# Two experts in halves of 128 rows: four output buffers, gathers spread over more gaps, fillers on TensorE ahead of three halves

## The chip, the cores and the metric

The kernel runs on one core of one Trainium2 chip. The metric is the device time of one execution in microseconds (us); lower is better. All times below are from runs and from one profiled execution of the kernel before.

## What is computed

The input x has 2 sequences of 1024 tokens with 128 channels. A layer norm, a two-level wavelet transform with linear attention, and a residual sum give x1. A second layer norm gives the rows h, on which a mixture of 16 experts and one shared expert work. The change touches the experts alone:

```
scores = sigmoid(h @ gate_w.T);  cap = ceil(T / E * TOP_K)   # T = 2048, E = 16, cap = 256
topk_score, topk_ids = top_k(scores.T, cap)                  # each expert picks 256 tokens
xin = h[topk_ids]
up = xin @ up_w.T + up_b;  g = xin @ gw.T + gb               # 128 -> 512, in 4 pieces of 128
eo = (silu(g) * up) @ down_w.T + down_b                      # 512 -> 128
out = zeros.at[topk_ids].add(eo * topk_score);  x = x + out + shared
```

Everything is fp32. An expert picks its own 256 tokens, so that two experts can have the same token: their sums into the output must not run at once.

## The kernel before

The kernel is written out by engine; each engine works through its own list in order, and semaphores order the engines. The first part (wavelet, attention, norms, the choice of 256 tokens for each expert, the shared expert) leaves a table h_rows in HBM (128 channels and 16 scores for each token), a table of row numbers in SBUF (rows, 2 x 128 for each expert), and the output in HBM with x and the shared expert's part.

Then come the experts. For expert e:

- GpSimd (POOL) issues two indirect DMAs that gather 128 rows each into gath (`gather(e, c)`, L525), c = 0 and 1. There are 7 buffers (GBUF); s_gath of the buffer counts both.
- TensorE (PE) turns the two chunks (`turn_x`, L1396) into a PSUM bank; VectorE (DVE) copies the 128 x 256 result to SBUF (`keep_x`, L1065).
- Four pieces j of 128 hidden features, numbered q = 4e + j through all experts: TensorE makes up (L1439) and gate (L1440), 256 columns each, ScalarE (ACT) the silu (L736), VectorE the product with the up part (L1091), and TensorE, two pieces later (LAG), the down product of each chunk (`down(q)`, L1414).
- VectorE adds the bias into eo (`add_bias`, L1075), ScalarE multiplies each chunk by the token's score (`weigh`, L560), and POOL issues two indirect DMAs that add the rows into the output (`scatter(e)`, L536).

eo has two buffers; `add_bias(e)` waits until scatter e-2 has landed. `scatter(e)` waits until scatter e-1 has landed.

In the steady part `turn_x(e+1)` stands in the middle of expert e (after j = 2), so that TensorE goes from one expert to the next without a gap. Only the last expert is different: at q = FINAL (60) TensorE first does the last two downs of expert 14, then `turn_x(15)`, and VectorE does `add_bias(14)` and `keep_x(15)` there.

The order on POOL is written out by hand: 12 gathers (experts 0 to 5), and then scatter 0, BETWEEN[0] gathers, scatter 1, BETWEEN[1] gathers, and so on. With the old BETWEEN (2 seven times, 1 six times, 0) the gathers of expert 13 stand behind scatters 7 and 8, those of expert 14 behind scatters 9 and 10, and those of expert 15 behind scatters 11 and 12.

`stay_warm(n, bank)` (L1112) issues n matmuls of 128 columns of the identity matrix into a bank that nobody reads; each fp32 matmul is two instructions in the trace, here as everywhere.

Of the kernel before, what the change touches and what calls it, by code (L numbers as in the profile page):

```python
# [11 lines left out]
ALU = mybir.AluOpType  # L12
# [9 lines left out]
P = 128  # L22
# [5 lines left out]
def wavelet_attention_moe(nc, x, packed, weights, shared, down_b, out):  # L28
# [21 lines left out]
    with ctx:  # L50
# [6 lines left out]
        def sem(name):  # L57
            return ctx.enter_context(nc.semaphore(name))
# [90 lines left out]
        eo = carve(2 * CH * C).rearrange("p (s c d) -> p s c d", s=2, c=CH)  # L149
# [14 lines left out]
        def up_bank(q):  # L164

            return UP_BANKS[q % len(UP_BANKS)]
# [115 lines left out]
        s_spread = sem("s_spread")  # L282
        s_rows = sem("s_rows")
        s_gath = [sem(f"s_gath{i}") for i in range(GBUF)]
        s_xsT = sem("s_xsT")
        s_xs = sem("s_xs")
        s_gu = sem("s_gu")
# [114 lines left out]
        def _(pool):  # L402
# [122 lines left out]
            def gather(e, c):  # L525
                if c == 0:
                    for g, (e0, _) in enumerate(GROUPS):
                        if e == e0:
                            pool.wait_ge(s_rows, g + 1)
                if e >= GBUF and c == 0:  # L530
                    pool.wait_ge(s_eo, CH * (e - GBUF + 1))
                pool.indirect_dma_start(out=gath[:, e % GBUF, c, :], out_offset=None, in_=h_rows[:, :],  # L532
                                        in_offset=bass.IndirectOffsetOnAxis(ap=rows[:, c, e:e + 1], axis=0),
                                        ).then_inc(s_gath[e % GBUF], 16)

            def scatter(e):  # L536
                if e == 0:
                    pool.wait_ge(s_store, 16 * (NT // 4))
                else:
                    pool.wait_ge(s_scat, 16 * CH * e)  # L540
                for c in range(CH):
                    pool.wait_ge(s_eo, CH * e + c + 1)
                    pool.indirect_dma_start(out=out_rows, in_=eo[:, e % 2, c, :], in_offset=None,  # L543
                                            out_offset=bass.IndirectOffsetOnAxis(ap=rows[:, c, e:e + 1], axis=0),
                                            compute_op=ALU.add).then_inc(s_scat, 16)

# [10 lines left out]
                    gather(*divmod(chunk, CH))  # L557
                    chunk += 1

        def weigh(act, e):  # L560

            act.wait_ge(s_eb, e + 1)
            for c in range(CH):
                act.activation(eo[:, e % 2, c, :], eo[:, e % 2, c, :], ACT.Copy,  # L564
                               scale=gath[:, e % GBUF, c, C + e:C + e + 1]).then_inc(s_eo, 1)


# [1 line left out]
        def _(act):  # L569
# [156 lines left out]
            for part in (0, 2):  # L726
                keep_shared(LAST, part)

            for q in range(E * FT):
                e, j = divmod(q, FT)  # L730
                if q == FINAL:
                    weigh(act, e - 1)
                act.wait_ge(s_gu, q + 1)
                if q >= SGB:
                    act.wait_ge(s_hid, q - SGB + 1)
                act.activation(sgate_e[:, q % SGB, :], up_bank(q)[:, CAP:2 * CAP], ACT.Silu,  # L736
                               bias=biasT[:, 1, j, e:e + 1]).then_inc(s_sil, 1)
                if q == FT or j == 2 and 1 < e < E - 1:
                    weigh(act, e - 1)
            weigh(act, E - 1)  # L740


        @block.vector
        def _(dve):
# [317 lines left out]
            slot_rows(1)  # L1062
            add_shared(LAST, bank[6])

            def keep_x(e):  # L1065
                dve.wait_ge(s_xsT, e + 1)
                if e >= 2:
                    dve.wait_ge(s_gu, FT * (e - 1))
                dve.tensor_copy(xselT[:, e % 2, :], bank[5 if e else 3][:, 0:CAP]).then_inc(s_xs, 1)  # L1069
# [5 lines left out]
            def add_bias(e):  # L1075
                dve.wait_ge(s_dn, e + 1)
                if e >= 2:
# [5 lines left out]
            for q in range(E * FT):  # L1083
                e, j = divmod(q, FT)
# [4 lines left out]
                if e >= 2:  # L1089
                    dve.wait_ge(s_dn, e - 1)  # L1090
                dve.scalar_tensor_tensor(hidden[:, e % 2, j, :], up_bank(q)[:, 0:CAP], biasT[:, 0, j, e:e + 1],  # L1091
                                         sgate_e[:, q % SGB, :], ALU.add, ALU.mult).then_inc(s_hid, 1)
                if q == FT or j == 1 and 1 < e < E - 1:
                    add_bias(e - 1)
                if 1 <= q < 1 + len(LATER):
                    piece, quarter = LATER[q - 1]
                    last = piece(2, quarter * NT // 4, (quarter + 1) * NT // 4)
                    if piece is hot_lo:
                        link(last)
                if q == 13:  # L1100
                    lay_table(2)
                if q == 16:
                    slot_rows(2)
                if j == 2 and e + 1 < E - 1:
                    keep_x(e + 1)
            add_bias(E - 1)


        @block.tensor
        def _(pe):  # L1110
# [282 lines left out]
            spread(1)  # L1393
            stay_warm(WARM_E, bank[7])

            def turn_x(e):  # L1396
                pe.wait_ge(s_gath[e % GBUF], 16 * CH * (e // GBUF + 1))
                if e:
                    pe.wait_ge(s_xs, e)
                if e == 1:  # L1400
                    pe.wait_ge(s_rows, 2)
                if e == 4:
                    pe.wait_ge(s_spreadL, 3)
                if e == 5:
                    pe.wait_ge(s_rows, 3)
                for c in range(CH):
                    last = pe.transpose(bank[5 if e else 3][:, c * P:(c + 1) * P], gath[:, e % GBUF, c, 0:C], ident[:, :])
                last.then_inc(s_xsT, 1)

            turn_x(0)  # L1410
# [1 line left out]
            LAG = 2  # L1412

            def down(q):  # L1414
                e, j = divmod(q, FT)
                pe.wait_ge(s_hid, q + 1)
                if j == 0 and e >= 2:
                    pe.wait_ge(s_eb, e - 1)
                for c in range(CH):
                    last = pe.matmul(bank[3 + e % 2][:, c * P:(c + 1) * P], hidden[:, e % 2, j, c * P:(c + 1) * P],  # L1420
                                     wT[:, e, 2, j, :], start=(j == 0 and c == 0), stop=(j == FT - 1),
                                     skip_group_check=True)
                if j == FT - 1:
                    last.then_inc(s_dn, 1)

            for q in range(E * FT):
                e, j = divmod(q, FT)
                if q == FINAL:
                    down(q - LAG)
                    down(q - 1)  # L1430
                    turn_x(E - 1)
                if j == 0:
                    pe.wait_ge(s_wT[e], 16)
                    pe.wait_ge(s_xs, e + 1)
                if q == 3:
                    pe.wait_ge(s_lastbase, 2)
                if q >= len(UP_BANKS):
                    pe.wait_ge(s_hid, q - len(UP_BANKS) + 1)
                pe.matmul(up_bank(q)[:, 0:CAP], wT[:, e, 0, j, :], xselT[:, e % 2, :], start=True, stop=True)  # L1439
                pe.matmul(up_bank(q)[:, CAP:2 * CAP], wT[:, e, 1, j, :], xselT[:, e % 2, :], start=True,  # L1440
                          stop=True).then_inc(s_gu, 1)
                if q == FT:
                    down(q - LAG)
                    down(q - 1)
                elif q >= LAG and q not in (FT + 1, FINAL, FINAL + 1):
# [5 lines left out]
                if j == 2 and e + 1 < E - 1:  # L1451
                    turn_x(e + 1)
            for q in range(E * FT - LAG, E * FT):
                down(q)


# [42 lines left out]
```

## Time and profile before

| | us |
|---|---|
| median of 3 runs | 206.62 (205.88 to 206.64) |
| the profiled execution's own time | 206.66 |
| span of the profiled execution | 204.9 |
| PE busy | 181.7 (89%) |
| POOL busy | 125.5 (61%) |
| DVE busy | 126.0 (61%) |
| ACT busy | 92.0 (45%) |
| mean granted TensorE clock | 0.966 of full |

The span goes from the first to the last event of the profile; the profiled execution's time is 1.76 us longer than its span. Times in rows count from the start of the span. A busy POOL is here a POOL that writes the descriptors of an indirect DMA; the transfer itself comes later.

### The profile page before, as it was taken

How to read it: one execution, taken by the hardware profiler on the slowest of the kernel's cores; microseconds unless marked ns; L12 is line 12 of the kernel's file. 1: busy time of each engine (PE TensorE's matmuls, PEld its weight loads, DVE VectorE, ACT ScalarE, POOL GpSimd, SP SyncE). 2: the span in 40 equal slices, each digit the busy share in tenths (PEclk: the TensorE clock that was granted, in tenths of full speed). 3: DMA queues.
4: the chain of work that ended last, by engine and by line, in shares of the span. 5: the costliest groups of instructions: out<-in, count | busy, mean ns of one | idle time of the engine just before them, and what ended most of it. 6: DMA issues, size and time to landing. Idle time of an engine off the chain costs nothing.

```text
span 204.9 us, 3617 instructions
## 1 busy us (share of the span) xinstructions
PE 181.7 (89%) x1196; PEld 156.7 (76%) x1196; DVE 126.0 (61%) x430; ACT 92.0 (45%) x240; POOL 125.5 (61%) x191
## 2 busy tenths in 40 slices
PE   6989889999979999998999999999999997948800
PEld 6957679998936577857889999999999996936700
DVE  3989999999777787784667654445444543421300
ACT  2476613468697767210344334444444454331210
POOL 7592006455126475937776888878887777775560
PEclk9999999999999999999999999999999999995875
DMA  5699999700030361114214223233232233332211
GB/s 168 214 408 420 421 419 417 321 4 3 0 117 0 109 214 51 53 31 144 75 44 57 27 42 53 46 40 42 42 58 33 36 40 43 40 40 26 26 13 13
DMA packets 11649, 22.26 MB, mean 109 GB/s; under 512 B 1504, under 2 KB 8800, under 8 KB 11504
## 3 DMA queue, kind: packets, MB, share of 16 engines
q1 hardware_dynamic: 5968, 17.52, 22.4%
q0 software_dynamic: 5664, 4.53, 16.0%
q8 instruction: 9, 0.15, 0.3%
q14 instruction: 8, 0.07, 0.1%
HBM read 17.72 MB, written 4.33 MB: 108 GB/s over the span
## 4 chain that ended last, share of the span: by engine, by line
PE 46%; POOL 13%; DVE 10%; issue 10%; DMA 10%; ACT 6%; POOLq 1%; SPq 0%; ACTq 0%; DVEq 0%
POOL out_dram L543 9%; PE bank L1160 7%; PE bank L1439 7%; PE bank L1440 6%; DMA out_dram<-area,rows 5%; PE bank L1420 5%; PE bank L1115 4%; POOL hT L532 4%; PE bank L1301 4%; PE bank L1313 3%; DMA hT<-h_rows,rows 3%; DMA x_tok<-in_x_dram 2%; PE bank L1263 1%; DVE junk L955 1%; DVE area L812 1%
## 5 line engine op out<-in xcount | busy, mean ns | idle before, releaser
L543 POOL DMA_INDIRECT out_dram<-area,rows x32 | 50.6, 1581 | 17.5 <-issue 6.8
L1091 DVE SCALAR_TENSOR_TENSOR area<-bank,consts,sgate 128x256 f32<-128x256 f32 x64 | 30.9, 483 | 43.4 <-ACT sgate L736 43.3
L736 ACT ACTIVATE sgate<-bank,consts 128x256 f32<-128x256 f32 x64 | 30.3, 474 | 56.4 <-PE bank L1440 56.2
L1439 PE MATMUL bank<-area,wT 128*128 128x256 f32 x128 | 40.2, 397 | 1.2 <-DVE area L1069 0.6
L1420 PEld LDWEIGHTS bank<-wT,area 128*128 128x128 f32 x256 | 38.1, 191 | 3.9 <-DVE area L1091 0.8
L532 POOL DMA_INDIRECT hT<-h_rows,rows x32 | 31.7, 990 | 12.7 <-issue 9.1
L1440 PE MATMUL bank<-area,wT 128*128 128x256 f32 x128 | 39.3, 390 | 0.0
L1420 PE MATMUL bank<-wT,area 128*128 128x128 f32 x256 | 38.6, 275 | 0.4 <-DVE area L1091 0.4
L1440 PEld LDWEIGHTS bank<-area,wT 128*128 128x128 f32 x128 | 25.2, 197 | 3.7
L519 POOL TENSOR_TENSOR sh_hid<-sh_up,sgate 128x64 f32<-128x64 f32 x48 | 13.6, 322 | 15.0 <-ACT sh_up L688 12.4
L1439 PEld LDWEIGHTS bank<-area,wT 128*128 128x128 f32 x128 | 20.5, 198 | 2.7 <-issue 2.2
L1115 PE MATMUL bank<-ident 128*128 128x128 f32 x132 | 19.4, 305 | 1.6 <-POOL ident L412 1.6
L1115 PEld LDWEIGHTS bank<-ident 128*128 128x128 f32 x132 | 18.0, 217 | 2.1 <-POOL ident L412 1.6
L1160 PE MATMUL bank<-sh_hid,area 128*128 128x128 f32 x160 | 18.6, 276 | 0.0
L1160 PEld LDWEIGHTS bank<-sh_hid,area 128*128 128x128 f32 x160 | 18.2, 192 | 0.4 <-ACT area L611 0.3
L1301 PE MATMUL bank<-hT,sh_wT 128*128 128x512 f32 x32 | 17.3, 629 | 0.6 <-ACT hT L652 0.6
L564 ACT ACTIVATE area<-area,hT 128x128 f32<-128x128 f32 x32 | 11.0, 392 | 7.5 <-DVE area L1079 7.5
L955 DVE TENSOR_SCALAR_CACHE_REDUCE junk<-area,search 128x256 bf16<-128x256 f32 (+1 forms) x30 | 13.2, 478 | 1.3 <-ACT area L666 0.8
L492 POOL TENSOR_TENSOR x_tok<-x_tok,consts 128x128 f32<-128x128 f32 x4 | 3.2, 815 | 15.9 <-DVE area L878 15.9
L1313 PEld LDWEIGHTS bank<-sh_wT,sh_hid 128*128 128x128 f32 x64 | 8.4, 191 | 4.4 <-issue 3.3
L448 POOL TENSOR_TENSOR rstd<-var_eps,half_pow 128x4 f32<-128x4 f32 (+1 forms) x6 | 7.4, 1229 | 6.2 <-DVE var_eps L766 6.2
L1079 DVE TENSOR_TENSOR area<-bank,x_tok 128x256 f32<-128x256 f32 x16 | 6.7, 419 | 6.0 <-DMA out_dram<-area,rows 5.1
(196 smaller groups left out, 259.9 us busy)
## 6 DMA issues: line engine op xcount, KB each, us to landing
wT<-in_weights_dram SPq DMA_DIRECT2D x16, 768.0 KB, 16.4
h_rows<-hrow SPq DMA_DIRECT2D x2, 576.0 KB, 3.6
x_tok<-in_x_dram SPq DMA_DIRECT2D x4, 256.0 KB, 3.9
x_tok<-in_down_b_dram SPq DMA_DIRECT2D x1, 1024.0 KB, 6.1
out_dram<-x SPq DMA_DIRECT2D x4, 256.0 KB, 2.1
hT<-h_rows,rows POOLq DMA_INDIRECT x32, 2.6
out_dram<-area,rows POOLq DMA_INDIRECT x32
sh_wT<-in_shared_dram SPq DMA_DIRECT2D x1, 384.0 KB, 3.2
```

Source lines behind the costliest of these rows:

```text
L532: pool.indirect_dma_start(out=gath[:, e % GBUF, c, :], out_offset=None, in_=h_rows[:, :], in_offset=bass.IndirectOffsetOnAxis(ap=rows[:, c ...
L543: pool.indirect_dma_start(out=out_rows, in_=eo[:, e % 2, c, :], in_offset=None, out_offset=bass.IndirectOffsetOnAxis(ap=rows[:, c, e:e + 1 ...
L736: act.activation(sgate_e[:, q % SGB, :], up_bank(q)[:, CAP:2 * CAP], ACT.Silu, bias=biasT[:, 1, j, e:e + 1]).then_inc(s_sil, 1)
L955: last = dve.tensor_scalar(junk[:, k, :], keys, cand[:, k:k + 1], 0.0, ALU.is_ge, ALU.add, accum_out=cnt[:, k:k + 1])
L1091: dve.scalar_tensor_tensor(hidden[:, e % 2, j, :], up_bank(q)[:, 0:CAP], biasT[:, 0, j, e:e + 1], sgate_e[:, q % SGB, :], ALU.add, ALU.mul ...
L1115: pe.matmul(spare[:, 0:P], ident[:, :], ident[:, :], start=True, stop=True)
L1160: last = pe.matmul(dst, band[:, b, m0 + o:m0 + o + P], diag_c[:, d0 - 4 + k, :], start=False, stop=(d0 == 4 and o == 2), skip_group_check= ...
L1301: pe.matmul(bank[2 * kind + t][:, :], sh_wT[:, 2 * kind + t, :], rhs, start=True, stop=True).then_inc((s_shg, s_shu)[kind], 1)
L1313: last = pe.matmul(bank[6 if n == LAST else 4][:, t * P:(t + 1) * P], sh_hid[:, n % 2, k, t * P:(t + 1) * P], sh_wT[:, 4 + k, :], start=(k ...
L1420: last = pe.matmul(bank[3 + e % 2][:, c * P:(c + 1) * P], hidden[:, e % 2, j, c * P:(c + 1) * P], wT[:, e, 2, j, :], start=(j == 0 and c = ...
L1439: pe.matmul(up_bank(q)[:, 0:CAP], wT[:, e, 0, j, :], xselT[:, e % 2, :], start=True, stop=True)
L1440: pe.matmul(up_bank(q)[:, CAP:2 * CAP], wT[:, e, 1, j, :], xselT[:, e % 2, :], start=True, stop=True).then_inc(s_gu, 1)
```

## The change

Experts 0 to 13 stay whole; experts 14 and 15 become two blocks each, one for each chunk of 128 rows. A block goes through the same steps as an expert, with 128 columns in place of 256, and numbers b (0 to 17) and q = 4b + j take the place of the expert's. From block 14 on, the steps between two blocks stand in the order in which they stood ahead of the last expert: the last two downs of the block before, then `turn_x`. Ahead of blocks 15, 16 and 17 there are 8 `stay_warm` matmuls between the two. The second chunk of experts 14 and 15 has a gather semaphore of its own, so that a block waits only for its own chunk. eo has four buffers in place of two. BETWEEN is 2 six times, 1 eight times and 0 twice.

```diff
-    BETWEEN = (2, 2, 2, 2, 2, 2, 2, 1, 1, 1, 1, 1, 1, 0, 0, 0)
+    BETWEEN = (2, 2, 2, 2, 2, 2, 1, 1, 1, 1, 1, 1, 1, 1, 0, 0)
+    EOB = 4
+    HALVED = E - 2
...
-                                        ).then_inc(s_gath[e % GBUF], 16)
+                                        ).then_inc(s_gath2[e] if e >= HALVED and c else s_gath[e % GBUF], 16)
...
-        FINAL = (E - 1) * FT
+        WHOLE = tuple(range(CH))
+        BLOCKS = [(e, WHOLE) for e in range(HALVED)] + [(e, (c,)) for e in range(HALVED, E) for c in range(CH)]
+        WARM_B = {HALVED + 1: 8, HALVED + 2: 8, HALVED + 3: 8}
...
-            for q in range(E * FT):
-                e, j = divmod(q, FT)
-                if q == FINAL:
-                    weigh(act, e - 1)
+            for q in range(len(BLOCKS) * FT):
+                b, j = divmod(q, FT)
+                e, chunks = BLOCKS[b]
+                n = len(chunks) * P
+                if b >= HALVED and j == 0:
+                    weigh(act, b - 1)
...
-                act.activation(sgate_e[:, q % SGB, :], up_bank(q)[:, CAP:2 * CAP], ACT.Silu,
+                act.activation(sgate_e[:, q % SGB, 0:n], up_bank(q)[:, CAP:CAP + n], ACT.Silu,
...
-                if e >= 2:
-                    dve.wait_ge(s_scat, 16 * CH * (e - 1))
-                dve.tensor_tensor(eo[:, e % 2, :, :], bank[3 + e % 2][:, 0:CAP].rearrange("p (c d) -> p c d", c=CH),
-                                  down_b_bc[:, e, :].unsqueeze(1).to_broadcast([P, CH, C]), ALU.add).then_inc(s_eb, 1)
+                if e == 2:
+                    dve.wait_ge(s_hot, 8)
+                if e >= EOB:
+                    dve.wait_ge(s_scat, 16 * CH * (e - EOB + 1))
+                dve.tensor_tensor(eo[:, e % EOB, c0:c0 + n, :], bank[3 + b % 2][:, 0:n * C].rearrange("p (c d) -> p c d", c=n),
+                                  down_b_bc[:, e, :].unsqueeze(1).to_broadcast([P, n, C]), ALU.add).then_inc(s_eb, 1)
...
-                if q == FINAL:
-                    add_bias(e - 1)
-                    keep_x(e)
+                if b >= HALVED and j == 0:
+                    add_bias(b - 1)
+                    keep_x(b)
...
-            def turn_x(e):
-                pe.wait_ge(s_gath[e % GBUF], 16 * CH * (e // GBUF + 1))
+            def turn_x(b):
+                e, chunks = BLOCKS[b]
+                if chunks == WHOLE:
+                    pe.wait_ge(s_gath[e % GBUF], 16 * CH * (e // GBUF + 1))
+                elif chunks[0] == 0:
+                    pe.wait_ge(s_gath[e % GBUF], 16 * CH * (e // GBUF) + 16)
+                else:
+                    pe.wait_ge(s_gath2[e], 16)
...
-                if q == FINAL:
+                if b >= HALVED and j == 0:
                     down(q - LAG)
                     down(q - 1)
-                    turn_x(E - 1)
+                    stay_warm(WARM_B.get(b, 0), up_bank(q))
+                    turn_x(b)
...
-                pe.matmul(up_bank(q)[:, 0:CAP], wT[:, e, 0, j, :], xselT[:, e % 2, :], start=True, stop=True)
-                pe.matmul(up_bank(q)[:, CAP:2 * CAP], wT[:, e, 1, j, :], xselT[:, e % 2, :], start=True,
+                pe.matmul(up_bank(q)[:, 0:n], wT[:, e, 0, j, :], xselT[:, b % 2, 0:n], start=True, stop=True)
+                pe.matmul(up_bank(q)[:, CAP:CAP + n], wT[:, e, 1, j, :], xselT[:, b % 2, 0:n], start=True,
                           stop=True).then_inc(s_gu, 1)
...
-                if j == 2 and e + 1 < E - 1:
-                    turn_x(e + 1)
+                if j == 2 and b + 1 < HALVED:
+                    turn_x(b + 1)
```

The remaining lines of the diff put b and n in place of e and 256 in the same way.

## Rows read from the trace of the kernel before

**Rows 1.** The chain that ended last: start us, us, what.

```profile
170.94 2.64 DMA hT<-h_rows,rows
...
194.27 0.44 DVE area L1079
...
195.89 1.55 POOL out_dram L543
```

**Rows 2.** Timeline of POOL: start us, us, what, idle before and its releaser.

```profile
146.44 1.58 POOL L543 DMA_INDIRECT out_dram<-area,rows  x1 [0.30 <-issue]
...
150.93 1.63 POOL L543 DMA_INDIRECT out_dram<-area,rows  x1 [0.30 <-issue]
...
165.60 1.02 POOL L532 DMA_INDIRECT hT<-h_rows,rows  x1 [0.30 <-issue]
...
185.53 1.55 POOL L543 DMA_INDIRECT out_dram<-area,rows  x1 [0.30 <-issue]
189.12 1.55 POOL L543 DMA_INDIRECT out_dram<-area,rows  x1 [2.04 <-DMA out_dram<-area,rows]
...
197.75 1.55 POOL L543 DMA_INDIRECT out_dram<-area,rows  x1 [0.30 <-issue]
```

**Rows 3.** Timeline of PE where experts 13, 14 and 15 begin.

```profile
166.93 0.38 PE L1407 MATMUL bank<-ident,hT 128*128 128x128 f32 x2
...
173.63 0.44 PE L1407 MATMUL bank<-ident,hT 128*128 128x128 f32 x2 [1.07 <-DMA hT<-h_rows,rows]
...
181.25 0.71 PE L1420 MATMUL bank<-wT,area 128*128 128x128 f32 x4 [0.19 <-DVE area L1091]
184.56 0.69 PE L1407 MATMUL bank<-ident,hT 128*128 128x128 f32 x2 [2.59 <-DMA hT<-h_rows,rows]
```

**Rows 4.** Timeline of PE, ACT and DVE in the last expert.

```profile
185.29 0.42 DVE L1069 COPY area<-bank 128x256 f32<-128x256 f32 x1 [1.39 <-PE bank L1407]
...
185.81 1.19 PE L1439 MATMUL bank<-area,wT 128*128 128x256 f32 x2 [0.56 <-issue]
...
190.96 0.61 PE L1420 MATMUL bank<-wT,area 128*128 128x128 f32 x4
...
191.41 0.60 PE L1439 MATMUL bank<-area,wT 128*128 128x256 f32 x2
...
191.84 0.59 PE L1440 MATMUL bank<-area,wT 128*128 128x256 f32 x2
...
192.47 0.47 ACT L736 ACTIVATE sgate<-bank,consts 128x256 f32<-128x256 f32 x1 [0.84 <-PE bank L1440]
192.98 0.48 DVE L1091 SCALAR_TENSOR_TENSOR area<-bank,consts,sgate 128x256 f32<-128x256 f32 x1 [0.82 <-ACT sgate L736]
...
193.52 0.71 PE L1420 MATMUL bank<-wT,area 128*128 128x128 f32 x4 [0.19 <-DVE area L1091]
...
194.73 0.69 ACT L564 ACTIVATE area<-area,hT 128x128 f32<-128x128 f32 x2 [1.78 <-DVE area L1079]
```

**Rows 5.** Timeline of PE: six stay_warm matmuls and the instruction behind them.

```profile
63.19 1.58 PE L1115 MATMUL bank<-ident 128*128 128x128 f32 x12
64.61 0.17 PE L1288 MATMUL bank<-cnt,same_bf 128*128 128x3 bf16 x1
```

**Rows 6.** Groups by line and shape: count, busy us, mean ns of one, idle before.

```profile
L564 ACT ACTIVATE area<-area,hT 128x128 f32<-128x128 f32 x32 | 11.0, 392 | 7.5 <-DVE area L1079 7.5
...
L908 DVE SCALAR_TENSOR_TENSOR x<-bank,sum_var,consts 128x128 f32<-128x128 f32 x16 | 4.6, 340 | 0.0
...
L1026 DVE TENSOR_TENSOR area<-bank,pick 128x128 f32<-128x128 f32 x1 | 0.3, 292 | 0.0
```

**Rows 7.** Windows: length, busy us and count of each engine, PEclk, DMA share, GB/s.

```profile
30.00:32.00 2.00, 1.23 (x6) 1.06 (x6) 1.86 (x5) 0.39 (x2) 0.00 (x0) 1.00 0.99 406
...
184.00:185.00 1.00, 0.44 (x2) 0.29 (x2) 0.00 (x0) 0.62 (x2) 1.00 (x1) 0.51 0.02 5
...
190.00:191.00 1.00, 1.00 (x4) 0.79 (x4) 0.48 (x1) 0.07 (x1) 0.70 (x2) 0.58 0.00 0
```

More of the change, by code:

```diff
@@ L284, in wavelet_attention_moe @@
         s_gath = [sem(f"s_gath{i}") for i in range(GBUF)]
+        s_gath2 = {e: sem(f"s_gath2_{e}") for e in range(HALVED, E)}
         s_xsT = sem("s_xsT")
@@ L542, in scatter @@
                     pool.wait_ge(s_eo, CH * e + c + 1)
-                    pool.indirect_dma_start(out=out_rows, in_=eo[:, e % 2, c, :], in_offset=None,
+                    pool.indirect_dma_start(out=out_rows, in_=eo[:, e % EOB, c, :], in_offset=None,
                                             out_offset=bass.IndirectOffsetOnAxis(ap=rows[:, c, e:e + 1], axis=0),
@@ L558, in _, with weigh @@
                     chunk += 1
[L560 to L564, printed above, removed]
+        def weigh(act, b):
+            e, chunks = BLOCKS[b]
+            act.wait_ge(s_eb, b + 1)
+            for c in chunks:
+                act.activation(eo[:, e % EOB, c, :], eo[:, e % EOB, c, :], ACT.Copy,
                                scale=gath[:, e % GBUF, c, C + e:C + e + 1]).then_inc(s_eo, 1)
@@ L735, in _ @@
                     act.wait_ge(s_hid, q - SGB + 1)
-                act.activation(sgate_e[:, q % SGB, :], up_bank(q)[:, CAP:2 * CAP], ACT.Silu,
+                act.activation(sgate_e[:, q % SGB, 0:n], up_bank(q)[:, CAP:CAP + n], ACT.Silu,
                                bias=biasT[:, 1, j, e:e + 1]).then_inc(s_sil, 1)
-                if q == FT or j == 2 and 1 < e < E - 1:
-                    weigh(act, e - 1)
-            weigh(act, E - 1)
+                if q == FT or j == 2 and 1 < b < HALVED:
+                    weigh(act, b - 1)
+            weigh(act, len(BLOCKS) - 1)
         @block.vector
@@ L1063, in _, with keep_x @@
             add_shared(LAST, bank[6])
-            def keep_x(e):
-                dve.wait_ge(s_xsT, e + 1)
-                if e >= 2:
-                    dve.wait_ge(s_gu, FT * (e - 1))
-                dve.tensor_copy(xselT[:, e % 2, :], bank[5 if e else 3][:, 0:CAP]).then_inc(s_xs, 1)
+            def keep_x(b):
+                n = len(BLOCKS[b][1]) * P
+                dve.wait_ge(s_xsT, b + 1)
+                if b >= 2:
+                    dve.wait_ge(s_gu, FT * (b - 1))
+                dve.tensor_copy(xselT[:, b % 2, 0:n], bank[5 if b else 3][:, 0:n]).then_inc(s_xs, 1)
@@ L1082, in _, with add_bias @@
-            dve.wait_ge(s_db_in, 16)
-            for q in range(E * FT):
-                e, j = divmod(q, FT)
-                if q == FINAL:
-                    add_bias(e - 1)
-                    keep_x(e)
-                dve.wait_ge(s_sil, q + 1)
[L1089 to L1094, printed above, removed]
+            def add_bias(b):
+                e, chunks = BLOCKS[b]
+                c0, n = chunks[0], len(chunks)
+                dve.wait_ge(s_dn, b + 1)
+                if e == 2:
[4 more added lines that the diff above has]
+                                  down_b_bc[:, e, :].unsqueeze(1).to_broadcast([P, n, C]), ALU.add).then_inc(s_eb, 1)
@@ new lines, in _ @@
+            dve.wait_ge(s_db_in, 16)
+            for q in range(len(BLOCKS) * FT):
+                b, j = divmod(q, FT)
+                e, chunks = BLOCKS[b]
+                n = len(chunks) * P
+                if b >= HALVED and j == 0:
+                    add_bias(b - 1)
+                    keep_x(b)
+                dve.wait_ge(s_sil, q + 1)
+                if b >= 2:
+                    dve.wait_ge(s_dn, b - 1)
+                dve.scalar_tensor_tensor(hidden[:, b % 2, j, 0:n], up_bank(q)[:, 0:n], biasT[:, 0, j, e:e + 1],
+                                         sgate_e[:, q % SGB, 0:n], ALU.add, ALU.mult).then_inc(s_hid, 1)
+                if q == FT or j == 1 and 1 < b < HALVED:
+                    add_bias(b - 1)
@@ L1103, in _ @@
                     slot_rows(2)
-                if j == 2 and e + 1 < E - 1:
-                    keep_x(e + 1)
-            add_bias(E - 1)
+                if j == 2 and b + 1 < HALVED:
+                    keep_x(b + 1)
+            add_bias(len(BLOCKS) - 1)
         @block.tensor
@@ L1394, in _ @@
             stay_warm(WARM_E, bank[7])
-            def turn_x(e):
-                pe.wait_ge(s_gath[e % GBUF], 16 * CH * (e // GBUF + 1))
-                if e:
-                    pe.wait_ge(s_xs, e)
-                if e == 1:
+            def turn_x(b):
+                e, chunks = BLOCKS[b]
+                if chunks == WHOLE:
[4 more added lines that the diff above has]
+                    pe.wait_ge(s_gath2[e], 16)
+                if b:
+                    pe.wait_ge(s_xs, b)
+                if b == 1:
                     pe.wait_ge(s_rows, 2)
-                if e == 4:
+                if b == 4:
                     pe.wait_ge(s_spreadL, 3)
-                if e == 5:
+                if b == 5:
                     pe.wait_ge(s_rows, 3)
-                for c in range(CH):
-                    last = pe.transpose(bank[5 if e else 3][:, c * P:(c + 1) * P], gath[:, e % GBUF, c, 0:C], ident[:, :])
+                for i, c in enumerate(chunks):
+                    last = pe.transpose(bank[5 if b else 3][:, i * P:(i + 1) * P], gath[:, e % GBUF, c, 0:C], ident[:, :])
                 last.then_inc(s_xsT, 1)
@@ L1414, in down @@
             def down(q):
-                e, j = divmod(q, FT)
+                b, j = divmod(q, FT)
+                e, chunks = BLOCKS[b]
                 pe.wait_ge(s_hid, q + 1)
[L1417 to L1421, printed above, removed]
+                if j == 0 and b >= 2:
+                    pe.wait_ge(s_eb, b - 1)
+                for i in range(len(chunks)):
+                    last = pe.matmul(bank[3 + b % 2][:, i * P:(i + 1) * P], hidden[:, b % 2, j, i * P:(i + 1) * P],
+                                     wT[:, e, 2, j, :], start=(j == 0 and i == 0), stop=(j == FT - 1),
                                      skip_group_check=True)
@@ L1424, in down @@
                     last.then_inc(s_dn, 1)
-            for q in range(E * FT):
-                e, j = divmod(q, FT)
-                if q == FINAL:
+            for q in range(len(BLOCKS) * FT):
+                b, j = divmod(q, FT)
+                e, chunks = BLOCKS[b]
+                n = len(chunks) * P
+                if b >= HALVED and j == 0:
                     down(q - LAG)
                     down(q - 1)
-                    turn_x(E - 1)
+                    stay_warm(WARM_B.get(b, 0), up_bank(q))
+                    turn_x(b)
                 if j == 0:
                     pe.wait_ge(s_wT[e], 16)
-                    pe.wait_ge(s_xs, e + 1)
+                    pe.wait_ge(s_xs, b + 1)
                 if q == 3:
@@ L1444, in _ @@
                     down(q - 1)
-                elif q >= LAG and q not in (FT + 1, FINAL, FINAL + 1):
+                elif q >= LAG and q != FT + 1 and not (b >= HALVED and j < LAG):
                     down(q - LAG)
@@ L1450, in _ @@
                     spread(2)
-                if j == 2 and e + 1 < E - 1:
-                    turn_x(e + 1)
-            for q in range(E * FT - LAG, E * FT):
+                if j == 2 and b + 1 < HALVED:
+                    turn_x(b + 1)
+            for q in range(len(BLOCKS) * FT - LAG, len(BLOCKS) * FT):
                 down(q)
```

5 lines of the change are left out of this document (1 added, 4 removed).

## The prediction

> **What bounds the kernel now.** I read the chain of waits backwards from the end first. It ends with the last two scatters on POOL; they wait for the weigh of expert 15, that for `add_bias(15)` on VectorE, and that for the last down on TensorE [rows 1]. Further back it goes through the matmuls of expert 15 to a gather, then through expert 14 to another gather (issued at 170.94) [rows 1]. So near the end two things take turns: POOL, which issues gathers between scatters, and TensorE, which works up what was gathered.
>
> Next I read POOL's timeline. A scatter waits until the one before it has landed: the second DMA of scatter 13 starts at 185.53, the first of scatter 14 at 189.12, 3.59 us later [rows 2]. That wait stands in seven gaps, those behind scatters 7 to 13, where one gather or none stands. Scatter 7 starts at 150.93 and scatter 14 at 189.12, so one of these gaps makes 38.19 / 7 = 5.46 us for each expert [rows 2]. Behind scatters 0 to 6 two gathers stand and POOL issues without a wait (idle 0.30 by "issue"); there POOL's own work is the period.
>
> Then TensorE's timeline. It is full until expert 14: `turn_x(13)` at 166.93 waits for nothing. `turn_x(14)` at 173.63 waited 1.07 us for its gather. The last down of expert 14 begins at 181.25, and `turn_x(15)` at 184.56 waited 2.59 us for its gather [rows 3]. In the windows the granted clock is 0.51 (1.2 GHz) in 184 to 185 and is only rising again in 190 to 191 (0.58) [rows 7]. So the end pays for late gathers twice, in waits and in a stretch at the lower of the two clock levels. This is what the change can win.
>
> **POOL's part.** Up to scatter 6 nothing changes. Behind it one gather stands in place of two, so scatter 7 no longer waits for POOL but for the landing: 146.44 + 3.59 = 150.03 in place of 150.93, a gain of 0.90. The later gaps have one gather as before; the new gather behind scatter 13 lies under the landing wait (idle 2.04 at 189.12 [rows 2], against 1.02 + 0.30 for a gather). So all later scatters could start 0.90 earlier: scatter 14 at 188.22 and, with 197.75 - 195.89 = 1.86 for one DMA [rows 1, 2], its second at 190.08, scatter 15 at 190.08 + 3.59 = 193.67 and its second at 195.53. That is POOL's bound: 2.22 us ahead of the 197.75 of before.
>
> The gathers, on the other hand, move one gap back. The second of expert 13 now takes the place that held 165.60: 164.70. A gather needs 2.69 us to the turn (170.94 to 173.63 [rows 1, 3]), so `turn_x(13)` can start at 167.39, 0.46 after the 166.93 at which it was wanted. That is a new wait; behind it in TensorE's list stands all the rest. The gathers of blocks 15, 16 and 17 come behind scatters 11, 12 and 13. Scatter 13's second DMA is at 184.63, the gather behind it at 186.49, its rows at 189.18; the two before are about 5.46 and 10.9 earlier, 183.7 and 178.3.
>
> **The buffers.** With four eo buffers `add_bias(e)` waits for scatter e-4 to land, where its wait for e-2 held VectorE before. TensorE had no gap from that wait up to expert 13, so I count nothing. The new wait on s_hot is for VectorE's own earlier work, and costs nothing.
>
> **TensorE's part.** From `turn_x` of an expert in the middle of the one before to the end of that next expert's last down there are (181.25 + 0.71) - 173.63 = 8.33 us, with nothing waited for [rows 3]. Expert 13 therefore ends at 167.39 + 8.33 = 175.72.
>
> Now the blocks. Nothing in the trace is a half block, but each operation of one has a near row. A matmul of 128 columns takes 0.11 for each of its two instructions (190.96 to 191.41 is four, 0.45 [rows 4]): 0.44 for up and gate, 0.22 for a down. The result is there 0.16 after the pace (0.61 - 0.45). ACT starts 0.04 after that (191.84 + 0.59 to 192.47), VectorE 0.04 after ACT, TensorE 0.06 after VectorE (193.46 to 193.52) [rows 4]. For 128 columns I take 0.39 for the silu (the weigh [rows 6]; above by 0.47, the 256-column silu), 0.34 for the product (L908, below by 0.29, above by 0.48), 0.29 for `keep_x` and `add_bias` (L1026, above by 0.42) [rows 4, 6].
>
> From the first up of a half: three up-gate pairs end at 1.32; the first hidden piece is ready at 0.44 + 0.16 + 0.04 + 0.39 + 0.04 + 0.34 + 0.06 = 1.47; down 0 to 1.69, pair 3 to 2.13, down 1 to 2.35. Pair 3's hidden piece is ready at 2.13 + 1.03 = 3.16, and down 3 ends at 3.38, its result 0.16 later. Ahead of the first up: one transpose (0.38 - 0.11 = 0.27), 0.04, `keep_x` 0.29, and 0.10 until the matmul (185.71 to 185.81 [rows 4]): 0.70. A half is thus 4.08, of which more than a quarter is latency, since the next half is not turned until this one's last down is issued.
>
> Block 14 has no fillers, but `add_bias(13)` (0.42) stands ahead of `keep_x` on VectorE: first up at 175.72 + 0.04 + 0.42 + 0.04 + 0.29 + 0.10 = 176.61, last down at 179.99.
>
> The fillers: twelve instructions took 64.61 - 63.19 = 1.42 [rows 5], so 8 matmuls (16 instructions) take 1.89. They stand ahead of `turn_x` in a list that TensorE works through in order, so their price is nothing only while the gather is out. TensorE comes to block 15 at 179.99 and its rows are there since 178.3; so this filler is paid in full, and each later one too: block 16 is reached at 185.96 (rows at 183.7), block 17 at 191.93 (rows at 189.18). Each block is 1.89 + 4.08 = 5.97, longer than the 5.46 in which POOL delivers.
>
> Block 17's last down is issued at 179.99 + 3 x 5.97 = 197.90, its result at 198.06. Then `add_bias` to 198.39, weigh of its one chunk to 198.82, and 0.77 until the scatter (194.73 + 0.39 = 195.12 to 195.89 [rows 1, 4]): 199.59. POOL's 195.53 has long passed. Before, this DMA started at 197.75. The tail behind it is unchanged: 204.9 - 197.75 = 7.15.
>
> **The sum**, made against the profiled execution (span 204.9, own time 206.66, 0.04 over the median): 199.59 - 197.75 = +1.84, so span 206.7 and time 208.5, 0.9% over the median of 206.62. About 0.5%, 1.03 us, is what a measurement of this kernel can tell from no change.
>
> The bounds: fillers at 0.11 an instruction instead of 0.118 (-0.3), no wait at expert 13 (-0.46), POOL 0.47 behind the weigh as after its second chunk before (-0.3), product at 0.29 (-0.2): -1.3, time 207.2. The 256-column durations for all of ACT and VectorE: +0.21 in each half (0.08 and 0.14, once each), 0.13 for `keep_x` in each: with the last `add_bias` and weigh +1.5, time 210.0.
>
> **Rivals.** (1) *POOL binds instead, faster.* If the fillers cost nothing, block 15 ends at 184.07 and block 16 at 188.15; block 17 waits for its rows at 189.18, ends at 193.4, and its scatter is ready at 195.0, before POOL's 195.53. Then the time is 206.66 - 2.22 = 204.4. For it: the gathers and the bare halves fit each other closely, no late gather costs 2.59 any more, and the slow stretch is gone. Against: by the rows the rows of x are there 2 to 3 us before each filler. It decides where the chain of halves is shorter by 4.1 in all; from 2.9 on (0.7 in each of the four) the kernel is faster by over 0.5%.
>
> (2) *No change that can be measured.* The chain is shorter than my sum by 0.8 to 2.9, through the lower bounds above and a little more: 205.6 to 207.6.
>
> (3) *The clock falls in the halves.* In a half with fillers TensorE works 1.89 + 0.22 + 1.76 + 0.88 = 4.75 of 5.97 us and has idle moments of up to 0.8. Before, 1.23 busy of 2.00 left the clock at 1.00, and the 2.59 of idle ahead of 184.56 is what stood before the fall [rows 3, 7]. If it falls as it did then, for some 6.6 us (184 to 190.6), 0.8 of 3.3 is lost: +2.6, time 211.1. The Trainium skill ("TensorE: Matmul & The Clock Gate", section "A second HAM failure mode: psum-queue depth-cycling") says that frequent short idle times between groups of matmuls can make the clock swing between its two levels. By that rule the halves are such a case and this rival's time holds; the window at 30 to 32, with its 1.00, does not bear it out.
>
> **How the numbers follow.** My sum, with its bounds: 0.61, of which 0.14 lies below 207.65 and counts as no change. Rival 1: 0.18. Rival 2 beyond my bounds: 0.10. Rival 3: 0.11. So faster 0.18, no change 0.24, slower 0.58. The likeliest is 208.5, with its own range 207.2 to 210.0. For 8 in 10 I reach down to rival 1 and leave out rival 3 and the uppermost part of my own bounds: 204.3 to 209.7.
>
> **What would show it.** Right: scatter 7 near 150.0 with the landing wait in front; `turn_x(13)` waiting about half a microsecond; no wait for a gather at blocks 15 to 17; some 1.9 of fillers ahead of each; about 6.0 from block to block at clock 1.00; first DMA of scatter 15 near 193.7, and the second waiting on ACT for 4 us behind it. Wrong: a wait for a gather ahead of blocks 16 or 17 (then POOL binds), halves much under 4 us, a clock of 0.5 among them, or the second DMA of scatter 15 close behind the first.

## The result, and the profile after

The changed kernel takes 209.62 us (median of 4 runs, 209.29 to 211.38), the kernel before 206.25 in the same comparison (4 runs): ratio 1.0204, 95% interval 1.015 to 1.0258. It is slower: by 2.0% by this ratio of the comparison, by 1.6% (3.37 us) by the two medians. The forecast was slower by 0.9%, 208.5. Between the two profiled executions the forecast was +1.84 us, and it came to 209.58 - 206.66 = +2.92.

The lines after are those of the changed kernel: the gather is L537, the scatter L548, `turn_x` L1428, up and gate L1464 and L1465, down L1442, silu L744, weigh L570, the fillers L1130. First POOL's timeline, which answers to [rows 2]: scatter 7, the second gather of expert 13, the second DMA of scatter 14 and the two DMAs of scatter 15.

```profile
149.98 1.59 POOL L548 DMA_INDIRECT out_dram<-area,rows  x1 [0.74 <-DMA out_dram<-area,rows]
...
164.71 1.02 POOL L537 DMA_INDIRECT hT<-h_rows,rows  x1 [0.30 <-issue]
...
189.86 1.56 POOL L548 DMA_INDIRECT out_dram<-area,rows  x1 [0.30 <-issue]
194.90 1.55 POOL L548 DMA_INDIRECT out_dram<-area,rows  x1 [3.48 <-ACT area L570]
200.54 1.55 POOL L548 DMA_INDIRECT out_dram<-area,rows  x1 [4.09 <-ACT area L570]
```

POOL did what the sum said until the halves: scatter 7 at 149.98 (forecast 150.03), the gather at 164.71 (164.70). From scatter 15 on it waits for ACT, thus for the halves: its first DMA starts at 194.90 (forecast 193.7), its second at 200.54, where it was 197.75 before. The tail behind it is 207.7 - 200.54 = 7.16, as before (7.15). What leads to this last DMA is the last down, `add_bias` and weigh:

```profile
199.01 0.49 PE L1442 MATMUL bank<-wT,area 128*128 128x128 f32 x2 [0.40 <-DVE area L1106]
...
199.54 0.29 DVE L1092 TENSOR_TENSOR area<-bank,x_tok 128x128 f32<-128x128 f32 x1 [0.58 <-PE bank L1442]
199.86 0.40 ACT L570 ACTIVATE area<-area,hT 128x128 f32<-128x128 f32 x1 [1.29 <-DVE area L1092]
```

Then the timeline of PE, which answers to [rows 3]: expert 13's turn, and of blocks 15 and 16 the last down of the block before and the fillers, and of block 15 the turn, the first up and gate, and the first down with the up behind it.

```profile
168.24 0.44 PE L1428 MATMUL bank<-ident,hT 128*128 128x128 f32 x2 [1.29 <-DMA hT<-h_rows,rows]
...
180.65 0.49 PE L1442 MATMUL bank<-wT,area 128*128 128x128 f32 x2 [0.40 <-DVE area L1106]
...
180.97 1.95 PE L1130 MATMUL bank<-ident 128*128 128x128 f32 x16
...
182.76 0.27 PE L1428 MATMUL bank<-ident,hT 128*128 128x128 f32 x1
...
183.46 0.46 PE L1464 MATMUL bank<-area,wT 128*128 128x128 f32 x2 [0.43 <-issue]
183.76 0.39 PE L1465 MATMUL bank<-area,wT 128*128 128x128 f32 x2
...
184.99 0.49 PE L1442 MATMUL bank<-wT,area 128*128 128x128 f32 x2
185.31 0.39 PE L1464 MATMUL bank<-area,wT 128*128 128x128 f32 x2
...
186.77 0.49 PE L1442 MATMUL bank<-wT,area 128*128 128x128 f32 x2 [0.40 <-DVE area L1106]
...
187.09 1.95 PE L1130 MATMUL bank<-ident 128*128 128x128 f32 x16
```

Two waits for rows became one: that of expert 13, 1.29 us long. No turn of a half waits for a gather. The fillers stand in full between a block's last down and the next turn, and from last down to last down it is 186.77 - 180.65 = 6.12 us.

The windows of PE's clock, which answer to [rows 7], cover the four halves (columns as there; the engines are PE, PEld, DVE, ACT and POOL):

```profile
176.00:182.00 6.00, 4.95 (x39) 4.41 (x40) 2.31 (x7) 2.57 (x7) 4.65 (x4) 1.00 0.37 42
182.00:188.00 6.00, 5.17 (x43) 4.63 (x42) 1.99 (x6) 1.85 (x5) 4.17 (x4) 1.00 0.31 38
188.00:194.00 6.00, 5.17 (x43) 4.63 (x42) 1.99 (x6) 1.75 (x6) 3.11 (x2) 1.00 0.29 34
194.00:200.00 6.00, 4.67 (x36) 3.94 (x34) 1.99 (x6) 1.75 (x6) 1.55 (x1) 1.00 0.12 11
```

The granted clock is 1.00 (2.4 GHz) all through, where it stood at 0.51 before. So the change does what it does at the places where it was made: no late gathers at the end, no slow stretch. It pays more for that than it wins.

### The profile page after: what moved, and what is told of

Same layout as the page of the kernel before. It is cut to its first block, busy times and chain, and to the rows that moved or that the text cites. A ratio compares the mean times of both kernels' runs of the same rounds, so it can differ in the third digit from the quotient of the medians.

```text
span 207.7 us, 3822 instructions
## 1 busy us (share of the span) xinstructions
PE 186.5 (90%) x1276; PEld 161.5 (78%) x1276; DVE 128.3 (62%) x442; ACT 94.2 (45%) x248; POOL 125.4 (60%) x191
## 4 chain that ended last, share of the span: by engine, by line
PE 49%; POOL 12%; DVE 11%; issue 10%; DMA 8%; ACT 6%; POOLq 1%; DVEq 0%; ACTq 0%
POOL out_dram L548 7%; PE bank L1464 7%; PE bank L1175 7%; PE bank L1465 6%; PE bank L1442 6%; PE bank L1130 6%; DMA out_dram<-area,rows 5%; PE bank L1316 4%; PE bank L1328 3%; POOL hT L537 3%; DMA hT<-h_rows,rows 2%; POOL rstd L453 2%; DMA x_tok<-in_x_dram 1%; PE bank L1278 1%; DVE junk L963 1%
## 5 line engine op out<-in xcount | busy, mean ns | idle before, releaser
L548 POOL DMA_INDIRECT out_dram<-area,rows x32 | 50.6, 1580 | 20.4 <-ACT area L570 8.5
L1106 DVE SCALAR_TENSOR_TENSOR area<-bank,consts,sgate 128x256 f32<-128x256 f32 (+1 forms) x72 | 32.7, 454 | 45.2 <-ACT sgate L744 44.3
L744 ACT ACTIVATE sgate<-bank,consts 128x256 f32<-128x256 f32 (+1 forms) x72 | 32.4, 450 | 58.8 <-PE bank L1465 58.1
L1464 PE MATMUL bank<-area,wT 128*128 128x256 f32 (+1 forms) x144 | 40.3, 362 | 2.6 <-issue 1.9
L1442 PEld LDWEIGHTS bank<-wT,area 128*128 128x128 f32 x256 | 37.9, 191 | 6.0 <-DVE area L1106 2.7
L1442 PE MATMUL bank<-wT,area 128*128 128x128 f32 x256 | 40.2, 278 | 1.8 <-DVE area L1106 1.8
L1465 PE MATMUL bank<-area,wT 128*128 128x256 f32 (+1 forms) x144 | 39.5, 356 | 0.0
L537 POOL DMA_INDIRECT hT<-h_rows,rows x32 | 31.7, 990 | 12.7 <-issue 9.1
L1465 PEld LDWEIGHTS bank<-area,wT 128*128 128x128 f32 x144 | 26.1, 190 | 2.9
L1130 PE MATMUL bank<-ident 128*128 128x128 f32 x180 | 25.0, 295 | 1.6 <-POOL ident L417 1.6
L1464 PEld LDWEIGHTS bank<-area,wT 128*128 128x128 f32 x144 | 22.0, 191 | 4.1 <-issue 4.0
L1130 PEld LDWEIGHTS bank<-ident 128*128 128x128 f32 x180 | 23.3, 208 | 2.1 <-POOL ident L417 1.6
L570 ACT ACTIVATE area<-area,hT 128x128 f32<-128x128 f32 x32 | 11.2, 392 | 7.9 <-DVE area L1092 7.9
L1078 DVE COPY area<-bank 128x256 f32<-128x256 f32 (+1 forms) x18 | 7.0, 389 | 6.3 <-PE bank L1428 6.3
```

Of the source, the lines that this page charges most:

```text
L548: pool.indirect_dma_start(out=out_rows, in_=eo[:, e % EOB, c, :], in_offset=None, out_offset=bass.IndirectOffsetOnAxis(ap=rows[:, c, e:e + ...
L744: act.activation(sgate_e[:, q % SGB, 0:n], up_bank(q)[:, CAP:CAP + n], ACT.Silu, bias=biasT[:, 1, j, e:e + 1]).then_inc(s_sil, 1)
L1106: dve.scalar_tensor_tensor(hidden[:, b % 2, j, 0:n], up_bank(q)[:, 0:n], biasT[:, 0, j, e:e + 1], sgate_e[:, q % SGB, 0:n], ALU.add, ALU.m ...
L1130: pe.matmul(spare[:, 0:P], ident[:, :], ident[:, :], start=True, stop=True)
L1442: last = pe.matmul(bank[3 + b % 2][:, i * P:(i + 1) * P], hidden[:, b % 2, j, i * P:(i + 1) * P], wT[:, e, 2, j, :], start=(j == 0 and i = ...
L1464: pe.matmul(up_bank(q)[:, 0:n], wT[:, e, 0, j, :], xselT[:, b % 2, 0:n], start=True, stop=True)
```

## The experiments

All ratios are to the kernel before, measured together with each experiment, with the 95% interval; times of different experiments come from different comparisons.

**1. No fillers** (e1). The theory after the result was that of the forecast: the fillers are paid in full, and the halves without them would keep the clock and leave POOL as the bound. The rival was that the fillers hold the clock.

```diff
-        WARM_B = {HALVED + 1: 8, HALVED + 2: 8, HALVED + 3: 8}
+        WARM_B = {}
```

> The changed kernel without the 24 fillers. Theory (each filler is paid in full, 1.9 us a block, and the clock holds without them): the halves follow each other every 4.2 us, block 17 waits for its rows until about 189, POOL's landing waits bind again; the second DMA of scatter 15 starts near 195.4 in place of 200.5, time about 204.4, and the clock stays at 1.00 until block 17. Rival (the fillers are what holds the clock): the granted clock falls to 0.5 somewhere in blocks 15 to 17, the halves take 6 us or more again, time 207 to 209.

205.21 us, ratio 0.996 (0.9921 to 0.9999). The windows of this run, each about one half:

```profile
176.50:181.00 4.50, 3.46 (x27) 2.92 (x26) 2.02 (x6) 2.16 (x6) 3.21 (x3) 1.00 0.25 31
181.00:185.40 4.40, 3.49 (x27) 2.95 (x27) 1.89 (x6) 1.87 (x5) 3.41 (x3) 1.00 0.40 46
185.40:189.80 4.40, 3.48 (x27) 2.95 (x27) 1.89 (x6) 1.87 (x5) 3.25 (x3) 1.00 0.24 34
189.80:194.20 4.40, 3.48 (x27) 2.94 (x26) 1.89 (x6) 1.87 (x5) 1.65 (x2) 1.00 0.36 34
```

TensorE is busy 3.5 of 4.4 us in a half and the clock stays at 1.00: the rival fell. The 24 fillers cost 209.62 - 205.21 = 4.4 us, and the clock does not need them. Two last downs in a row show what a half takes without them:

```profile
180.71 0.49 PE L1442 MATMUL bank<-wT,area 128*128 128x128 f32 x2 [0.39 <-DVE area L1106]
...
185.13 0.49 PE L1442 MATMUL bank<-wT,area 128*128 128x128 f32 x2 [0.39 <-DVE area L1106]
```

That is 4.42 us, against 6.12 with fillers: 1.70 for each eight, not 1.89. The last down of all comes 199.01 - 193.98 = 5.0 us earlier. Less of that came back at the end, since POOL now binds; its timeline there:

```profile
189.91 1.55 POOL L548 DMA_INDIRECT out_dram<-area,rows  x1 [0.30 <-issue]
194.10 1.55 POOL L548 DMA_INDIRECT out_dram<-area,rows  x1 [2.64 <-DMA out_dram<-area,rows]
195.95 1.55 POOL L548 DMA_INDIRECT out_dram<-area,rows  x1 [0.30 <-issue]
```

Scatter 15 waits for a landing again, not for ACT. It starts 4.19 behind the second DMA of scatter 14, not 3.6; experiments 5 and 9 and the last section come back to that.

**2. Twice the fillers** (e2).

```diff
-        WARM_B = {HALVED + 1: 8, HALVED + 2: 8, HALVED + 3: 8}
+        WARM_B = {HALVED + 1: 16, HALVED + 2: 16, HALVED + 3: 16}
```

> The changed kernel with 16 fillers ahead of each of the three halves in place of 8. Theory (paid in full): 3 x 1.9 = 5.7 us more than the changed kernel, about 215.3. Rival (part of the fillers lies under a wait for the rows, or under VectorE's add_bias and keep_x): clearly less, 211 to 213.

214.91 us, ratio 1.044 (1.0369 to 1.0511): 5.3 us over the changed kernel, where 5.7 was expected. From last down to last down:

```profile
180.70 0.49 PE L1442 MATMUL bank<-wT,area 128*128 128x128 f32 x2 [0.40 <-DVE area L1106]
...
188.60 0.49 PE L1442 MATMUL bank<-wT,area 128*128 128x128 f32 x2 [0.40 <-DVE area L1106]
```

That is 7.90 us, 1.78 more than 6.12, and three times 1.78 is 5.3. So nothing of the added fillers lies under another wait; eight of them are 1.78 long, not 1.89.

**3. The old order of gathers** (e3).

```diff
-    BETWEEN = (2, 2, 2, 2, 2, 2, 1, 1, 1, 1, 1, 1, 1, 1, 0, 0)
+    BETWEEN = (2, 2, 2, 2, 2, 2, 2, 1, 1, 1, 1, 1, 1, 0, 0, 0)
```

> The changed kernel with the old BETWEEN (gathers one gap earlier). Theory (the halves' chain on TensorE binds, and the move of the gathers costs it the wait at expert 13): turn_x(13) waits for nothing, the chain starts 1.3 us earlier, time 208.3. Rival (POOL's order has no part in it): 209.6 as the changed kernel.

208.10 us, ratio 1.0114 (1.0045 to 1.0183). Expert 13's turn starts without a wait,

```profile
166.70 0.38 PE L1428 MATMUL bank<-ident,hT 128*128 128x128 f32 x2
```

1.5 earlier than in the changed kernel, and the end moves by as much (the second DMA of scatter 15 is at 198.93). With fillers in place the new order gave the halves nothing; it cost them the wait at expert 13.

**4. The new order alone** (e4): the kernel before, with BETWEEN of the changed kernel.

> The kernel before with the new BETWEEN alone: no halves, two eo buffers, no fillers. Theory (whole experts need both chunks, and these now land one gap later): expert 14 starts near 178.2 in place of 173.6, expert 15 near 189 in place of 184.6, time about 211. Rival (the gathers have slack, the earlier scatters win): 206 or a little less.

214.72 us, ratio 1.0407 (1.0351 to 1.0463), nearly twice the loss expected. The profiled execution took 217.04, 2.3 over the median, and lagged by about 2 us from the first gather on (92.10 in place of 90.11), so its waits tell more than its times. The timeline of POOL shows the cause (L543 and L532 are scatter and gather of the kernel before): scatter 13, and the gather behind it.

```profile
188.87 1.58 POOL L543 DMA_INDIRECT out_dram<-area,rows  x1 [4.62 <-ACT area L564]
...
192.61 1.02 POOL L532 DMA_INDIRECT hT<-h_rows,rows  x1 [0.30 <-issue]
```

Expert 14 came late, as expected (its turn waited 4.27 us). But in the order of VectorE's list `add_bias(13)` stands inside expert 14, behind the product of its second piece. So scatter 13 waited 4.62 us for the weigh that follows it, and behind scatter 13 on POOL stands the last gather of expert 15, at 192.61 where 186.5 was counted on. Expert 15's turn then waited 4.82 us, and behind both waits the granted clock was about half (0.54 in 182 to 184, 0.50 in 196 to 200). I had moved the gather by its gap and forgotten what is queued ahead of it.

**5. Ten fillers fewer at the start** (e5). In the changed kernel one gather stands out: the second of expert 13. Time from issue to landing (min/median/max of this one), and the queues in 164.5 to 168.5:

```profile
DMA to landing us min/median/max: 3.5/3.5/3.5
```

```profile
q0 software_dynamic: 177, 0.14, 26.4%
q8 instruction: 1, 0.02, 1.5%
```

The gather before it, like most, took 2.6, and with the old order this gather itself takes 2.7. The one packet of the instruction queue takes 1.5% of 16 engines over 4 us, that is 0.96 us of one engine, and the gather is late by about as much. In e1, e2 and e4 this gather took 3.7 to 3.9. To move the packet without moving the gather, I took 40 instructions (ten matmuls, each two matmul and two weight-load instructions in the trace) away from TensorE's program ahead of everything:

```diff
-            stay_warm(18, bank[7])
+            stay_warm(8, bank[7])
```

> The changed kernel with 8 in place of 18 stay_warm matmuls at its very start, so that TensorE's program has 40 instructions less ahead of the experts. In the changed kernel the second gather of expert 13 took 3.5 us to land and not the 2.6 of its neighbours, and a 16 KB packet of the instruction queue stood in the same few microseconds. Theory (the fetch of instructions holds up the gather): the fetch moves by some 2.5 us, away from this gather, which lands after 2.6; turn_x(13) waits about 0.4 us in place of 1.3, and the time is some 0.9 lower, 208.7. Rival (this gather is slow at this place for its own sake, its rows or the traffic around it): it lands after 3.5 or more again, turn_x(13) waits 1.3, time 209.6.

208.60 us, ratio 1.015 (1.0104 to 1.0196), 1.0 less than the changed kernel. The gather of expert 13, issued at 164.60, landed after

```profile
DMA to landing us min/median/max: 2.6/2.6/2.6
```

with no packet of the instruction queue in its window, and the turn started at

```profile
167.24 0.44 PE L1428 MATMUL bank<-ident,hT 128*128 128x128 f32 x2
```

where the forecast had 167.39. The packets had moved: one now stood beside the second gather of expert 12, which took 3.8 in place of 2.6 (nobody waits for that one). The rival, that this gather is slow for its own sake, fell.

**6. Halves alone** (e6): as e3, and without fillers.

> The changed kernel without fillers and with the old BETWEEN: halves and four buffers alone. Theory (without fillers POOL's landing waits bind, with either order): turn_x(13) waits for nothing, the halves follow each other every 4.4 us, the second DMA of scatter 15 starts near 196, time 205.2, as without fillers in the new order. Rival (the new order is what won there): 206.5 or more.

205.85 us, ratio 1.002 (0.9988 to 1.0052). The halves follow each other every 4.42 us and POOL binds, as expected; the time lies between theory and rival, 0.6 over e1 in the median, with intervals that overlap. The second DMA of scatter 15 starts at 196.84. Scatter 14 started 4.46 us behind scatter 13's second DMA, with a packet of the instruction queue beside it; with 3.55, as in most of these gaps, I estimate 196 for the last. So with or without the new order the halves end within 1 us of each other, and halves with the old order win nothing that can be measured.

**7. Expert 15 alone halved** (e7): as e6 with HALVED = E - 1.

> As halves alone, but only expert 15 is halved (old BETWEEN, four buffers, no fillers). Theory (what the halves win is that the first half of expert 15 fills the wait for its second gather, and keeps the clock): TensorE never waits over 1 us behind expert 14, clock 1.00 until block 16, POOL binds, time 205.2, no worse than with both halved. Rival (expert 14 must be halved too): a wait of 2 us or more before expert 15, clock 0.5 behind it, 206.5.

204.83 us, ratio 0.9977 (0.9941 to 1.0013). The clock stays at 1.00 through both halves and POOL binds; the first half of expert 15 is enough to fill the wait. Expert 14's turn waits 1.22 us for its gather, a little over what I gave it.

**8. Four buffers alone** (e8): the kernel before with EOB = 4 and the waits of the changed kernel in `add_bias`.

> The kernel before with four eo buffers alone. Theory (VectorE's waits in add_bias held nobody): 206.6, no change, though the waits of 0.7 us are gone from VectorE's timeline. Rival (the buffers are worth something by themselves): 205.5 or less.

206.55 us against 206.09, ratio 1.0055 (1.0011 to 1.0098): no gain. VectorE's waits for scatters between 150 and 182 (2.9 us in four of them) are gone, and the time did not gain from it. The interval says slightly slower; three of its ten runs lie near 208.2, where one of 25 of the kernel before does (208.58). Its profile is of an execution of 205.35, one of its fastest, and shows nothing that would cost time, so I leave that open.

**9. No fillers at either place** (e9): e1 with the edit of e5.

> The changed kernel without its 24 fillers, and with 8 in place of 18 stay_warm matmuls at its very start. Without fillers POOL's landing waits bind; there the second DMA of scatter 14 took 4.2 us to the next scatter and not 3.6, and a packet of the instruction queue stood beside it. Theory (the fetch held up the scatter, and moves by some 2.5 us here): scatter 15 starts 3.6 us behind scatter 14's second DMA, turn_x(13) waits 0.4 us, time 204.3 to 204.6, ratio about 0.991. Rival (the last scatter is slow by itself): 4.2 again, 205.2.

205.38 us, ratio 0.9949 (0.9915 to 0.9983). In POOL's timeline scatter 15 now follows 3.52 behind the second DMA of scatter 14:

```profile
191.18 1.56 POOL L548 DMA_INDIRECT out_dram<-area,rows  x1 [0.30 <-ACT area L570]
194.70 1.55 POOL L548 DMA_INDIRECT out_dram<-area,rows  x1 [1.96 <-DMA out_dram<-area,rows]
```

and expert 13's turn waits 0.29. Both times are those of the theory. But at the scatter the packet did not leave the window: one started 1.08 us behind the second DMA of scatter 14, where it was 1.93 in e1 (the last section comes back to that). The time did not fall to 204.3. The profiled execution (205.57) was late from the first gather on (91.2 where e1 had 89.9, scatter 9 at 162.04 where e1 had 160.65); whether that is so in the others, and so in the median, no trace shows.

**10. Expert 15 alone halved, again** (e10): the kernel of e7, measured anew.

> The kernel with expert 15 alone halved, old order, four buffers, no fillers, once more and in more rounds, since its interval reached over 1. Theory (POOL binds, and the low clock behind expert 14 is gone): 204.8, ratio 0.995, an interval below 1. Rival (no gain): 206, ratio 1.000.

205.39 us, ratio 0.9972 (0.994 to 1.0004). The interval of this gain of 0.3% reaches over 1 twice, so the gain is not shown. Only the changed kernel without its fillers has intervals below 1 against the kernel before, by 0.4% (e1, just below) and 0.5% (e9, with fewer fillers at the start too). That is no more than the 0.5% that I had named as the least a measurement can tell, and in the medians e9 and e10 are level (205.38 and 205.39 in one comparison).

## Why the prediction was right in direction and wrong in size

- *Scatters start 0.90 earlier from scatter 7 on:* right (149.98 against 150.93).
- *The gathers of expert 13 come late and TensorE waits:* right in kind. The first step that failed is "A gather needs 2.69 us to the turn": here it took 168.24 - 164.71 = 3.53, because a packet of the instruction queue stood beside it (experiment 5). The wait was 1.29 in place of 0.46, and the turn came 168.24 - 167.39 = 0.85 later than summed, out of the 1.08 us that the forecast fell short of.
- *Fillers paid in full, 1.89 each:* right that they are paid, and a little too long. From their first instruction to the turn it is 182.76 - 180.97 = 1.79; eight more cost 1.78 (experiment 2), and without them a block is 1.70 shorter (experiment 1).
- *A half of 4.08, a block of 5.97:* 6.12. The second step that failed is "A matmul of 128 columns takes 0.11 for each of its two instructions", 0.22 in all. That holds in a row without a wait, but behind a wait the first up took 0.30 to the next (183.46 to 183.76), the first down 0.32 (184.99 to 185.31), and the last down 0.32 to the fillers (186.77 to 187.09). The shorter fillers make up for the last of these. From the first up to the last down it is 186.77 - 183.46 = 3.31, where 3.16 was counted, and these 0.15 are paid in each of four halves: 0.6 in all.
- *0.77 from weigh's end to the scatter, and the steps before it:* too much. From the last down of block 17 (199.01) to the scatter (200.54) it took 1.53 where the sum had 1.91: -0.38. The weigh ended at 200.26, and the scatter started 0.28 behind it, not 0.77. The first up of block 14 came 0.12 sooner behind expert 13's turn than summed. 0.85 + 0.60 - 0.38 - 0.12 = 0.95, and the scatter is indeed 200.54 - 199.59 = 0.95 late. The remaining 0.13 of the 1.08 lies outside the span, where this execution spent 209.58 - 207.7 = 1.88 and the one before 1.76.
- *POOL is not the bound:* right. Rival 1 (fillers cost nothing) is what the kernel does without them (experiment 1), except that the last landing wait there was 4.19 and not the 3.59 I took.
- *Rival 3, the clock falls in the halves:* wrong, and clearly so. The Trainium skill ("TensorE: Matmul & The Clock Gate", section "A second HAM failure mode: psum-queue depth-cycling") says that frequent short idle times between groups of matmuls can make the clock swing. In this case the halves without fillers, with 0.9 us of idle in every 4.4, left it at 1.00 (experiment 1); no swing shows in them.
- *The size.* The two failed steps are 0.85 and 0.60 of it, less the 0.38 and 0.12 above. By the medians the gap is wider still (3.37 us), because the kernel before came to 206.25 in that comparison and my sum stood on an execution of 206.66. That 209.62 lies inside my bounds (up to 210.0) is luck: they reached so far through longer durations on ACT and VectorE, and those did not come (in the halves the silu took 0.37 on the mean where I took 0.39, the product 0.35 for 0.34, the weigh 0.39 as taken). I had bounded the engines' durations and none of the DMAs. One gather of [rows 1] was my only row for landing times, though the trace of the kernel before held a slow one among its 32 gathers:

```profile
DMA to landing us min/median/max: 2.5/2.6/3.5
```

## What to carry to other kernels

A filler that keeps an engine warm costs nothing only while that engine would wait anyway: set it against the landing time of what it waits for, and look whether the clock falls without it, before paying for it. When a load is moved later, follow what its new place in the queue waits for in its turn; in experiment 4 a gather stood behind a scatter, the scatter waited for the next expert's work, and that expert waited for a late gather itself. And bound a transfer's landing by the slowest of its kind in the trace (3.5 us here), not by the one row at hand (2.6).

## What the runs showed that I had not expected

A fetch of instructions can hold up a gather by about a microsecond. In these traces most gathers landed in 2.5 to 2.7 us; the second gather of expert 13 took 3.5 to 3.9 in all four with the new order and the full start (the changed kernel, e1, e2, e4), each with one packet of the instruction queue in its window, and 2.6 in e5, without one. The packets' own times show the same beyond this gather. Of the 380 gathers with a recorded landing in the twelve traces, 17 have a packet of the 16 KB kind (queue q8) that starts 1.1 to 2.0 us behind the start of the gather's issue: these landed after 3.2 to 3.9 us. The 318 with no such packet beside them took 2.6 in the median and 3.3 at most; the 45 with one at another moment took 2.6 in the median and 3.5 at most. The slow gather of the kernel before, the first of expert 6, is one of the 17. The Trainium skill ("DMA: Bandwidth & Descriptors", section "Queues, rings and completion order") says that a DMA engine drains a whole packet of one queue before it turns to another; the same page ("Why a DMA increments its semaphore by 16 and not by 1") says that a transfer's semaphore counts engines which finish independently. By that rule one engine held for 0.96 us delays the whole gather, which agrees with the 0.9 that was measured. That it happens in this way is argued, not shown; which engine it was, no run here tells.

Scatters suffer alike, but only when the packet comes at the wrong moment. Three landing waits stand out in the twelve traces: 4.19 us (e1, scatter 14 to 15), 4.46 (e6, 13 to 14) and 4.55 (e2, 13 to 14), from a scatter's second DMA to the next scatter. In each a packet started 1.9 to 2.3 us behind that second DMA. With a packet 0.9 to 1.4 us behind it, as in e9 (1.08, and 3.52 to the next scatter), or 2.8 us and more, the wait is 3.7 at most, as it is without one. From e1 to e9 the packet of that window moved from 1.93 to 1.08, and the wait fell by 0.67. That is one pair of executions, so for scatters it is less well shown than for the gather. The packets follow the length of TensorE's program: 40 instructions fewer at its start moved those of the 16 KB kind by 1.5 to 4.8 us (the changed kernel against e5).
